# A three-layer graph network on one core: node update and second convolution taken in finished 512-node source chunks inside the edge loop

## The chip, the cores and the metric

One NeuronCore of one Trainium2 chip runs the whole program. The metric is the device time of one execution in microseconds; the runs shown are three, and one further execution was profiled.

## What is computed

3125 nodes of 128 features, 100000 edges sorted by destination, 64 features an edge. Four graph layers follow one another, each with a residual and a LayerNorm. The change concerns the two in the middle.

```python
# layer 1: message network over the edges, then node update
m_input = concat([x[src], x[dst], edge_attr])
h = relu(m_input @ W1 + b1)
messages = relu(h @ W2 + b2)
agg = segment_sum(messages, dst)
x = layernorm(x + layer_norm(x + relu(agg @ Wn + bn), gamma, beta))
# layer 2: convolution with self loops, norm = dinv[row] * dinv[col]
agg = segment_sum(norm * x[row], col)          # edges and one loop per node
x = layernorm(x + layer_norm(agg @ W.T + b, gamma, beta))
# layer 3: h = (1 + eps) * x + segment_sum(x[src], dst); h @ W.T + b; batch norm; relu; residual; layernorm
```

Layers 0, 2 and 3 sum over neighbours by a matrix `adj` of edge counts (25 source tiles of 128 nodes by 3200 destinations, bf16), which the kernel builds first. fp32 rows are split into three bf16 parts (high, middle, low) for these sums.

## The kernel before

The program runs in phases; `phase_end` makes all five engines meet. Every engine has its own instruction stream, written out by hand with semaphores between them.

**Phase 6, the edge loop** (layer 1). 196 blocks of 512 edges, four a loop iteration (`SLOTS`), on every engine a loop over iterations 1 to 47 with a peeled start and end. For each block GpSimd issues four gathers of 128 rows of x @ W1a (`gather`, L602 to L609); before them it waits for the block's index copy (VectorE, `gather_index`, L1446) and for the block four before to be through TensorE's transposes. TensorE's `step` (L865) does, for block b: `hidden_t(b+1)` (L834 transposes the gathered rows, L838 adds the edge part), `inputs_t(b+2)` (L825, transposes the edge features that SP loaded), `sum_nodes(b-1)` (L855), `messages(b)` (L845), `window(b-1)` (L863). ScalarE (`step`, L1124) does `hidden_relu(b+1)` (L1113), `inputs_out(b+2)` (L1108), `take_sums(b-1)` (L1122), `message_relu(b)` (L1117). VectorE (`step`, L1488) does `add_window(b-2)` (L1485: a window of 24 nodes is added into `agg_all`), `gather_index(b+3)`, `block_start(b+3)` (L1473) and `add_bias(b)` (L1479). At the head of each iteration VectorE and SP load four window bases into registers (`bases`). SP issues, per block, the load of 128 KB of edge features (`features`, L463) and a 12 KB load (L492), each once TensorE has used the buffer two blocks back.

**Phase 7** (node update and layer 2). SP loads bn and all of x1 (L510 to L514). TensorE updates seven chunks of 512 nodes (`update`, L902: agg @ Wn plus the bias by an identity matmul, two passes each), VectorE and ScalarE form the residual, two normalizations and the split (`residual`, `norm_1`, `residual_2`, `norm_2`, `less_hi`, `mid`, `less_mid`, L1550 to L1580 and L1156 to L1180), staggered over the chunks; GpSimd adds beta (L624). TensorE sums into the first three destination chunks as sources come (`begin_gcn`, L916), then runs the other four (`aggregate`, L718: 25 source tiles times three parts, 75 matmuls a chunk), adds the self term by transposes (`own_t`, L730, ScalarE copies it, VectorE adds it, L1607) and multiplies by the weight (`gcn`, L934). VectorE ends with node steps (L1617) and groups of two LayerNorms each (`gcn_norms`, L1622), over eight tiles at a time, then four, four and one. SP loads bias, gamma and beta of this layer when the last split is done (L515 to L518).

**Phase 8** is layer 3, with its self term scaled by 1 + eps on ScalarE.

If the input does not suit the windows, a flag (`general`) sends all engines into a fallback (`scan`). That is not taken with this input.

Of the kernel before, what the change touches and what calls it, by code (L numbers as in the profile page):

```python
# [19 lines left out]
F32 = mybir.dt.float32  # L20
# [6 lines left out]
P = 128  # L27
# [8 lines left out]
J = 4  # L36
# [13 lines left out]
SLOTS = 4  # L50
assert NT * WIN_A <= 512 and GRP % 2 == 0
# [9 lines left out]
def build(nc, t, out, x1_d, xa_d, xb_d, table_d):  # L61
    ctx = ExitStack()
    with ctx:
# [8 lines left out]
        arena = sb("arena", [P, 10112], F32)  # L72
# [24 lines left out]
        off = sb("off", [P, 9], F32)  # L97
# [38 lines left out]
        def edge(a, n):  # L136
# [5 lines left out]
        h_t = [edge(o + 2048 + 512 * u, 512) for u in range(2)]  # L142
        msg = edge(o + 3072, 512)
        assert o + 4096 <= 4800
        ec_t = arena[:, 8000:8512]
        w_e = [arena[:, 9024 + 128 * u:9152 + 128 * u] for u in range(2)]
        oh_e = [arena[:, 9280 + 96 * v:9376 + 96 * v].rearrange("p (j w) -> p j w", j=J)
                for v in range(SLOTS)]
        sums = [arena[0:WIN, 9792 + D * u:9792 + D * (u + 1)] for u in range(2)]
# [74 lines left out]
        sums_out = [sem(f"sums_out{v}") for v in range(SLOTS)]  # L224
        win_ready = [sem(f"win_ready{v}") for v in range(SLOTS)]
# [91 lines left out]
        BEGUN = 3  # L317

# [60 lines left out]
        def _(sp):  # L379
# [107 lines left out]

            def edge_loads(i, v, b, last=False):
# [8 lines left out]
            with sp.Else():  # L497
# [12 lines left out]
            sp.dma_start(bias_b[:, :], bcast(t["L1_gnn_bn"])).then_inc(bn_loaded, 16)  # L510
            for c, (k0, nt) in enumerate(CHUNKS):
                sp.dma_start(x1[c], x1_d[k0 * P:(k0 + nt) * P, :].rearrange("(k p) d -> p k d", p=P)
                             ).then_inc(x1_loaded[c > 0], 16)
            sp.dma_start(w_b[:, :], t["L2_gnn_W"]).then_inc(loads[7], 16)  # L514
# [33 lines left out]
        def _(pool):  # L548
# [71 lines left out]
            pool.wait_ge(update_loaded, 48)  # L620
            for c, (k0, nt) in enumerate(CHUNKS):
                x1_wait(pool, c)
                pool.wait_ge(lin_used, 2 * NC + c + 1)
                pool.tensor_tensor(x1[c], x1[c], over(beta_b, nt), ALU.add).then_inc(xb_ready, 1)  # L624
            with pool.If_ne(flag, 0):
                scan(pool, X2, scan_tile)
# [1080 lines left out]
```

## Time and profile before

| what | us |
|---|---|
| runs, median of 3 (lowest, highest) | 1943.5 (1942.7, 1945.01) |
| the profiled execution, its own time | 1940.99 |
| its span, first to last instruction | 1939.0 |
| edge loop, GpSimd's first to last gather | 610.3 to 1592.4 |
| phase 7, first DMA issue to that of phase 8 | 1604.98 to 1782.16 |
| mean granted TensorE clock | 0.967 of full |

Times in the rows are microseconds from the span's start unless marked ns. PE is TensorE's matmul side, PEld its weight loads, DVE VectorE, ACT ScalarE, POOL GpSimd, SP SyncE (SPq its queue); L12 is line 12 of the kernel. An fp32 matmul shows as two passes. What stands in brackets behind a row is how long the engine had been idle and what released it; "issue" is time in which it waited for nothing that the profile shows. Ends of matmuls are modelled.

### The profile page before, as it was taken

The numbers are of one execution on the slowest core, as the hardware profiler recorded it, in microseconds if no ns is written. First come the engines' busy times: TensorE is split into PE (matmuls) and PEld (weight loads), VectorE is DVE, ScalarE is ACT, GpSimd is POOL, SyncE is SP. The second block draws the span as 40 slices with busy tenths as digits, with TensorE's granted clock in tenths as the row PEclk, the third lists the DMA queues.
The fourth block names the chain that finished last, engine by engine and source line by source line (L and its number), as shares of the span: only waits on it lengthen the run. The fifth ranks groups of instructions, "written<-read, shape, count | busy, mean of one in ns | idle before, by whom it ended". The sixth has DMA issues, their size and how long they took to land.

```text
span 1939.0 us, 35472 instructions
## 1 busy us (share of the span) xinstructions
PE 1594.3 (82%) x10363; PEld 1041.1 (54%) x10364; DVE 731.2 (38%) x2702; ACT 692.8 (36%) x1413; POOL 767.6 (40%) x805
## 2 busy tenths in 40 slices
PE   2777777998996888888888888888888884994995
PEld 1444445544555666666666666666666663442444
DVE  7998893112233222222222222222222225365004
ACT  4666663002002443444444444444444445301001
POOL 3000000000003777777777777777777761000000
PEclk9999997999997999999999999999999996997998
DMA  1000000001005333333333333333333321000001
GB/s 54 0 0 0 0 0 3 1 1 38 0 1 141 88 80 82 81 81 81 82 81 80 82 82 80 81 81 81 82 81 82 80 67 38 5 1 2 1 0 34
DMA packets 158346, 93.71 MB, mean 48 GB/s; under 512 B 120529, under 2 KB 143824, under 8 KB 158296
## 3 DMA queue, kind: packets, MB, share of 16 engines
q0 software_dynamic: 25088, 51.43, 10.2%
q1 hardware_dynamic: 133208, 41.60, 8.8%
q8 instruction: 34, 0.56, 0.1%
q14 instruction: 16, 0.13, 0.0%
HBM read 86.44 MB, written 6.52 MB: 48 GB/s over the span
## 4 chain that ended last, share of the span: by engine, by line
POOL 26%; PE 18%; issue 17%; DMA 3%; DVE 3%; ACT 1%; SPq 1%; POOLq 0%; DVEq 0%; ACTq 0%
POOL arena L607 26%; PE ps L726 8%; PE ps L929 3%; DMA arena<-x_w1a,idx 2%; PE ps L845 1%; PE ps L855 1%; PE ps L838 1%; PE ps L834 1%; DVE arena L1335 1%; PE ps L825 1%; DMA x_w1b<-arena 0%; DVE stats L1325 0%; PE ps L863 0%; PE ps L939 0%; PE ps L960 0%
## 5 line engine op out<-in xcount | busy, mean ns | idle before, releaser
L607 POOL DMA_INDIRECT arena<-x_w1a,idx x784 | 740.6, 945 | 832.2 <-issue 824.2
L726 PE MATMUL ps<-adj,arena 128*128 (+2 forms) x1875 | 367.7, 358 | 14.6 <-DVE arena L1300 7.9
L726 PEld LDWEIGHTS ps<-adj,arena 128*128 128x128 bf16 x1875 | 172.1, 99 | 203.2 <-issue 26.0
L1473 DVE TENSOR_TENSOR arena<-win_i,drel 128x96 f32<-128x96 f32 x196 | 50.7, 259 | 554.7 <-PE ps L855 551.3
L1117 ACT ACTIVATE arena<-arena 128x512 f32<-128x512 f32 x196 | 123.6, 631 | 302.6 <-DVE arena L1479 302.6
L834 PE MATMUL ps<-ident_f,arena 128*128 128x128 f32 x784 | 126.7, 284 | 126.1 <-DMA arena<-x_w1a,idx 126.1
L845 PE MATMUL ps<-w_c,arena 128*128 128x128 f32 x1568 | 226.9, 288 | 0.0
L660 PE MATMUL ps<-arena 128*128 128x300 bf16 x784 | 164.8, 296 | 63.1 <-DVE arena L1287 63.1
L1113 ACT ACTIVATE arena<-ps,cols 128x512 f32<-128x512 f32 x196 | 134.8, 688 | 218.2 <-PE ps L838 218.2
L845 PEld LDWEIGHTS ps<-w_c,arena 128*128 128x128 f32 x1568 | 189.7, 191 | 40.1 <-issue 40.1
L855 PE MATMUL ps<-arena 128*24 128x128 f32 x1568 | 206.6, 275 | 2.2 <-ACT arena L1117 2.2
L838 PE MATMUL ps<-arena 88*128 88x512 f32 x392 | 201.8, 596 | 0.0
L1006 ACT ACTIVATE adj<-ps 128x300 f32 x392 | 166.7, 449 | 97.4 <-PE ps L665 91.5
L1287 DVE TENSOR_SCALAR arena<-arena 128x300 bf16<-128x300 int16 x784 | 179.6, 292 | 0.0
L1479 DVE TENSOR_TENSOR arena<-ps,bias_b 128x512 f32<-128x512 f32 x196 | 135.5, 691 | 110.5 <-PE ps L845 110.5
L855 PEld LDWEIGHTS ps<-arena 128*24 128x24 f32 x1568 | 145.5, 102 | 46.2 <-issue 36.7
L834 PEld LDWEIGHTS ps<-ident_f,arena 128*128 128x128 f32 x784 | 83.1, 141 | 144.4 <-issue 82.0
L825 PEld LDWEIGHTS ps<-ident_f,arena 128*88 128x88 f32 x784 | 91.2, 122 | 113.1 <-issue 113.1
L665 PE MATMUL ps<-adj,ident_h 128*128 x392 | 124.6, 318 | 6.7
L660 PEld LDWEIGHTS ps<-arena 128*128 128x128 bf16 x784 | 79.6, 115 | 89.8 <-DVE arena L1287 76.2
L825 PE MATMUL ps<-ident_f,arena 128*88 128x128 f32 x784 | 118.9, 274 | 6.3 <-DVE arena L1473 5.5
L1108 ACT ACTIVATE arena<-ps 88x512 f32<-88x512 f32 x196 | 114.0, 582 | 12.4 <-PE ps L825 8.6
(167 smaller groups left out, 1242.1 us busy)
## 6 DMA issues: line engine op xcount, KB each, us to landing
arena<-in_edge_attr SPq DMA_DIRECT2D x196, 128.0 KB, 2.2
arena<-x_w1a,idx POOLq DMA_INDIRECT x784
arena<-x_w1b SPq DMA_DIRECT2D x196, 12.0 KB
x_spill<-arena SPq DMA_DIRECT2D x1, 1600.0 KB, 7.7
x_w1a<-arena SPq DMA_DIRECT2D x6, 256.0 KB, 2.3
x_w1b<-arena SPq DMA_DIRECT2D x6, 256.0 KB, 2.4
arena<-x_spill SPq DMA_DIRECT2D x6, 256.0 KB, 4.6
out_x<-arena SPq DMA_DIRECT2D x3, 512.0 KB
```

What stands on the lines that cost most here:

```text
L607: pool.indirect_dma_start(out=z_e[v][:, j * D:(j + 1) * D], out_offset=None, in_=xa_d[:, :], in_offset=bass.IndirectOffsetOnAxis(ap=idx[:, ...
L660: last = pe.matmul(ps[:, q, 0:NT * WIN_A], oh_src[v][:, :, j], oh_dst[v][:, j, :], start=(j == 2 * h), stop=False)
L726: last = pe.matmul(ps[:, u, 0:w], parts[q][:, k, :], adj[:, k, bass.ds(c0, w)], start=(k == 0 and q == 0), stop=(k == NT - 1 and q == 2))
L825: last = pe.transpose(ps[0:KE, 0, j * P:(j + 1) * P], ec[v % 2][:, j, :], ident_f[:, :])
L834: pe.matmul(z_t[:, j * P:(j + 1) * P], z_e[v][:, j * P:(j + 1) * P], ident_f[:, :], is_transpose=True, start=(j == 0), stop=False)
L838: pe.matmul(z_t, w_e[v % 2][0:KE, :], ec_t[0:KE, :], start=False, stop=True).then_inc(z_ready[v], 1)
L845: last = pe.matmul(ps[:, 5, j * P:(j + 1) * P], h_t[v % 2][:, j * P:(j + 1) * P], w_c[:, :], start=True, stop=True)
L855: last = pe.matmul(ps[0:WIN, 1, 0:D], oh_e[v][:, j, :], msg[:, j * P:(j + 1) * P], start=(j == 0), stop=(j == J - 1))
L1006: act.activation(adj[:, :, bass.ds(b, WIN_A)], ps[:, q, 0:NT * WIN_A].rearrange("p (k w) -> p k w", w=WIN_A), ACT.Copy).then_inc(adj_writt ...
L1113: act.activation(h_t[v % 2], ps[:, 2 + v % 2, :], ACT.Relu, bias=cols[:, 0:1]).then_inc(h_ready[v], 1)
L1287: last = dve.tensor_scalar(oh_dst[v][:, j, :], iota_c, comb[:, bass.ds(s, 1), j], None, ALU.is_equal)
L1479: dve.tensor_tensor(msg.rearrange("p (j d) -> p j d", d=D), bank(5, J), over(bias_b, J), ALU.add).then_inc(m_sum[v], 1)
```

## The change

- In the loop the iterations are written as: eight plain ones, then five segments of eight (`SEG`; the last has seven), one for each of the first five chunks of 512 nodes, whose destinations no later block touches (`settled`, checked in the preparation by five one-element operations on VectorE that feed the flag). In a segment, iteration r = 0 makes the update of chunk c, iteration r = 1 finishes norms and split, and each of the following ones (r = 2; 29 in all) sums the chunk's four source tiles into one destination chunk u (`partial`: 12 matmuls of 512 columns, in thirds behind the second, third and fourth block). VectorE adds each result to `acc` in SBUF (`take_partial`). Destination chunk 6 (128 columns) is done in the next segment's r = 0.
- The update's x1 chunk comes through one buffer, loaded by SP in iteration r = 1 once VectorE has used the previous one.
- `h_t` and `sums` have one buffer instead of two; ScalarE's step has another order.
- Phase 7 keeps chunks 5 and 6 of the update, one after the other, then sums only those sources (and chunk 4 for destinations 5 and 6) by `gcn_sums`: 15 matmuls a destination, 27 for the last two. VectorE adds `acc` to each (`add_partials`). No self term: `loops` adds the identity to the diagonal blocks of `adj`. The old code stays behind the flag.
- Layer 3's self term is scaled by eps instead of 1 + eps.
- `arena` grows from 10112 to 13248 words a partition; the scratch of the software DMA is set to 4096.

```diff
+EARLY = 5
+SEG = 8
+SEG0 = 9
...
+        def blocks(eng, iteration):
+
+            with eng.Fori(1, SEG0) as i:
+                iteration(i)
+            for c in range(EARLY):
+                i0 = SEG0 + SEG * c
+                iteration(i0, c, 0)
+                iteration(i0 + 1, c, 1)
+                with eng.Fori(i0 + 2, min(i0 + SEG, NB // SLOTS - 1)) as i:
+                    iteration(i, c, 2, i - (i0 + 2))
...
-                with sp.Fori(1, NB // SLOTS - 1) as i:
+                sp.dma_start(w_b[:, :], bcast(t["L1_gnn_bn"])).then_inc(bn_loaded, 16)
+                x1_rows(0)
+
+                def iteration(i, c=None, r=None, u=None):
                     b = bases(sp, base_regs, i)
                     for v in range(SLOTS):
                         edge_loads(i, v, b[v])
+                    if r == 1:
+                        sp.wait_ge(xb_ready, c + 1)
+                        x1_rows(c + 1)
+
+                blocks(sp, iteration)
...
+            def update_tiles(c, some, bank, bias):
+
+                if some[0] == 0:
+                    if c == 0:
+                        pe.wait_ge(update_loaded, 48)
+                        pe.wait_ge(bn_loaded, 16)
+                    if c < EARLY:
+                        b = settled(c)
+                        pe.wait_ge(win_added[b % SLOTS], b // SLOTS + 1)
+                        pe.wait_ge(lin_used, 2 * NC + c)
+                for j in some:
+                    k = CHUNKS[c][0] + j
+                    o = ps[:, bank, j * D:(j + 1) * D]
+                    pe.matmul(o, agg_all[:, k * P:(k + 1) * P], w_a[:, :], start=True, stop=False)
+                    last = pe.matmul(o, ident_f[:, :], bias[:, :], start=False, stop=True)
+                if some[-1] == CHUNKS[c][1] - 1:
+                    last.then_inc(lin_ready, 1)
...
+            def partial(c, u, third):
+
+                w = P if isinstance(u, int) and u == NC - 1 else CH * P
+                if third == 0:
+                    pe.wait_ge(low_ready, 2 * NC + c + 1)
+                    pe.wait_ge(part_added, u + (NC * c + 1))
+                for n in range(4 * third, 4 * third + 4):
+                    j, q = n // 3, n % 3
+                    last = pe.matmul(ps[:, 6, 0:w], up_parts[c][q][:, j, :],
+                                     adj[:, CHUNKS[c][0] + j, bass.ds(u * (CH * P), w)],
+                                     start=(n == 0), stop=(n == 3 * CH - 1))
+                if third == 2:
+                    last.then_inc(part_sum, 1)
...
+                def iteration(i, c=None, r=None, u=None):
+                    for n in range(SLOTS):
+                        step(*at(i, n + 1))
+                        if r == 0 and n < 2:
+                            update_tiles(c, (2 * n, 2 * n + 1), 4, w_b)
+                        if r == 0 and c > 0 and n > 0:
+                            partial(c - 1, NC - 1, n - 1)
+                        if r == 2 and n > 0:
+                            partial(c, u, n - 1)
+
+                blocks(pe, iteration)
...
+                for c, bank in ((NC - 2, 2), (NC - 1, 3)):
+                    update_tiles(c, range(CHUNKS[c][1]), bank, w_b)
+                transposed_weight(loads[7], 16)
+                gcn_sums(0)
+                gcn_sums(1)
+                for u in range(NC):
+                    gcn(2, u, CHUNKS[u][1], sum_t[u % 2])
+                    if u + 2 < NC:
+                        gcn_sums(u + 2)
+                pe.sem_inc(self_ready, NC)
...
-                passed(act, m_ready, i, v, back=2)
-                act.activation(h_t[v % 2], ps[:, 2 + v % 2, :], ACT.Relu, bias=cols[:, 0:1]).then_inc(h_ready[v], 1)
+                passed(act, m_ready, i, v, back=1)
+                act.activation(h_t, ps[:, 2 + v % 2, :], ACT.Relu, bias=cols[:, 0:1]).then_inc(h_ready[v], 1)
...
             def step(i, v, left=2, first=False):
-                if left >= 1:
-                    hidden_relu(*at(i, v + 1))
                 if left >= 2:
                     inputs_out(*at(i, v + 2))
                 if not first:
                     take_sums(*at(i, v - 1))
+                if left >= 1:
+                    hidden_relu(*at(i, v + 1))
                 message_relu(i, v)
...
+            def up_norm_2(c):
+                k0, nt = CHUNKS[c]
+                norm_factors()
+                for j in range(nt):
+                    act.activation(xn[:, k0 + j, :], up_node[c][:, j, :], ACT.Identity,
+                                   scale=rstd[:, CH + j:CH + j + 1], bias=nbias[:, CH + j:CH + j + 1])
+                    last = act.activation(up_node[c][:, j, :], up_node[c][:, j, :], ACT.Identity,
+                                          scale=scaled[:, j:j + 1], bias=scaled[:, CH + j:CH + j + 1])
+                last.then_inc(xs_ready, 1)
+                act.wait_ge(xs_ready, c + 1)
+                if 0 < c < EARLY:
+                    act.wait_ge(part_sum, NC * c)
+                act.activation(up_parts[c][0], up_node[c], ACT.Copy).then_inc(hi_ready, 1)
...
+                def iteration(i, c=None, r=None, u=None):
+                    for n in range(SLOTS):
+                        step(*at(i, n + 1))
+                        if (r, n) == (0, 2):
+                            root(CH)
+                        if (r, n) == (0, 3):
+                            up_norm_1(c)
+                        if (r, n) == (1, 0):
+                            root(CH, CH)
+                        if (r, n) == (1, 1):
+                            up_norm_2(c)
+                        if (r, n) == (1, 2):
+                            up_mid(c)
+
+                blocks(act, iteration)
...
+            def loops(c):
+                for k in range(CHUNKS[c][0], CHUNKS[c][0] + CHUNKS[c][1]):
+                    own.add(dve.tensor_tensor(adj[:, k, k * P:(k + 1) * P], adj[:, k, k * P:(k + 1) * P], ident_h[:, :], ALU.add))
+
+            def up_residual(c, bank):
+                nt = CHUNKS[c][1]
+                dve.wait_ge(x1_loaded[0], 16 * (c + 1))
+                dve.wait_ge(lin_ready, 2 * NC + c + 1)
+                if c > 0:
+                    dve.wait_ge(low_ready, 2 * NC + c)
+                dve.scalar_tensor_tensor(out=up_node[c], in0=bank_of(bank, nt), scalar=0.0, in1=up_x1[c],
+                                         op0=ALU.max, op1=ALU.add).then_inc(lin_used, 1)
+                dve.wait_ge(lin_used, 2 * NC + c + 1)
+                own.add(dve.tensor_tensor(up_x1[c], up_x1[c], over(beta_b, nt), ALU.add))
+                statistics(c, 0, up_node[c])
...
+            def up_residual_2(c):
+                nt = CHUNKS[c][1]
+                dve.wait_ge(normed, c + 1)
+                own.add(dve.tensor_tensor(up_node[c], up_node[c], over(gamma_b, nt), ALU.mult))
+                own.wait()
+                dve.tensor_tensor(up_node[c], up_node[c], up_x1[c], ALU.add).then_inc(xb_ready, 1)
+                dve.wait_ge(xb_ready, c + 1)
+                statistics(c, CH, up_node[c])
...
+            def take_partial(c, u):
+
+                w = P if isinstance(u, int) and u == NC - 1 else CH * P
+                dst = acc[:, bass.ds(u * (CH * P), w)]
+                dve.wait_ge(part_sum, u + (NC * c + 1))
+                if c == 0:
+                    last = dve.tensor_copy(dst, ps[:, 6, 0:w])
+                else:
+                    last = dve.tensor_tensor(dst, dst, ps[:, 6, 0:w], ALU.add)
+                last.then_inc(part_added, 1)
...
+                        if (r, n) == (0, 0):
+                            loops(c)
+                        if (r, n) == (0, 2):
+                            up_residual(c, 4)
+                        if (r, n) == (0, 3):
+                            factors(c, 0)
+                            if c > 0:
+                                take_partial(c - 1, NC - 1)
+                        if (r, n) == (1, 0):
+                            up_residual_2(c)
+                        if (r, n) == (1, 1):
+                            factors(c, CH)
+                        if (r, n) == (1, 2):
+                            up_less_hi(c)
+                        if (r, n) == (1, 3):
+                            up_low(c)
+                        if (r, n) == (2, 3):
+                            take_partial(c, u)
+
+                blocks(dve, iteration)
...
+            with dve.Else():
+                dve.wait_ge(part_added, SUMS_DONE)
+                for c in range(EARLY, NC):
+                    loops(c)
+                    up_residual(c, 2 + c - EARLY)
+                    factors(c, 0)
+                    up_residual_2(c)
+                    factors(c, CH)
+                    up_less_hi(c)
+                    up_low(c)
+                dve.wait_ge(loads[8], 48)
+                gcn_all(add_partials, tail_node, 1)
...
-    nc = _bacc.Bacc("TRN2", target_bir_lowering=False, num_devices=1)
+    nc = _bacc.Bacc("TRN2", target_bir_lowering=False, num_devices=1, dynamic_dma_scratch_size=4096)
```

## Rows read from the trace of the kernel before

**Rows 1.** Busy time by stretch: us, then busy and count of PE, PEld, DVE, ACT, POOL, PE clock.
```profile
640.00:1600.00 960.00, 832.74 (x5376) 605.43 (x5374) 255.89 (x953) 395.87 (x768) 719.42 (x762) 1.00 0.32 80
...
1605.00:1640.00 35.00, 10.86 (x80) 10.67 (x80) 19.40 (x89) 15.75 (x42) 5.07 (x4) 0.65 0.19 52
```

**Rows 2.** Instructions in time order, inside the loop: start, us, engine, line, operation.
```profile
1116.28 0.94 POOL L607 DMA_INDIRECT arena<-x_w1a,idx  x1 [0.30 <-issue]
...
1118.14 0.69 DVE L1479 TENSOR_TENSOR arena<-ps,bias_b 128x512 f32<-128x512 f32 x1 [0.51 <-PE ps L845]
...
1118.84 0.16 DVE L1449 COPY idx<-src_idx 128x4 int32 x1
...
1118.94 0.66 PE L834 MATMUL ps<-ident_f,arena 128*128 128x128 f32 x4 [0.51 <-DMA arena<-x_w1a,idx]
...
1121.81 1.16 PE L845 MATMUL ps<-w_c,arena 128*128 128x128 f32 x8
...
1122.52 0.94 POOL L607 DMA_INDIRECT arena<-x_w1a,idx  x1 [0.30 <-issue]
...
1130.07 0.17 DVE L1449 COPY idx<-src_idx 128x4 int32 x1
...
1132.51 0.94 POOL L607 DMA_INDIRECT arena<-x_w1a,idx  x1 [0.30 <-issue]
```

**Rows 3.** The same view, TensorE in the loop's start-up.
```profile
630.46 0.60 PE L834 MATMUL ps<-ident_f,arena 128*128 128x128 f32 x4
...
634.69 0.66 PE L834 MATMUL ps<-ident_f,arena 128*128 128x128 f32 x4
```

**Rows 4.** The same view, the head of phase 7.
```profile
1604.98 0.36 SPq L510 DMA_DIRECT2D bias_b<-in_L_gnn_bn  x1
1605.38 5.07 SPq L512 DMA_DIRECT2D arena<-x_spill  x7
...
1614.59 0.80 PE L907 MATMUL ps<-w_a,arena 128*128 128x128 f32 x2 [10.02 <-issue]
...
1618.45 0.69 DVE L1556 SCALAR_TENSOR_TENSOR arena<-ps,arena 128x512 f32<-128x512 f32 x1 [13.55 <-PE ps L908]
...
1621.31 1.65 ACT L1159 ACTIVATE arena<-arena,nbias,rstd 128x128 f32<-128x128 f32 x4 [0.45 <-DVE nbias L1541]
```

**Rows 5.** The same view, sums and norms of phase 7.
```profile
1701.27 16.35 PE L726 MATMUL ps<-adj,arena 128*128 128x512 bf16 x75
1701.96 1.65 DVE L1325 BATCH_NORM_STATS2 stats<-arena 128x6 f32<-128x128 f32 x8
...
1715.95 0.69 DVE L1607 TENSOR_TENSOR arena<-ps,arena 128x512 f32<-128x512 f32 x1
...
1718.55 1.13 DVE L1617 SCALAR_TENSOR_TENSOR arena<-ps,dinv,bias_b 128x128 f32<-128x128 f32 x4 [1.91 <-PE ps L939]
...
1759.09 4.35 PE L726 MATMUL ps<-adj,arena 128*128 128x128 bf16 x75
...
1770.03 0.86 DVE L1325 BATCH_NORM_STATS2 stats<-arena 128x6 f32<-128x128 f32 x4
...
1778.22 0.29 DVE L1325 BATCH_NORM_STATS2 stats<-arena 128x6 f32<-128x128 f32 x1
...
1782.16 0.33 SPq L528 DMA_DIRECT2D w_b<-in_L_gnn_W  x1
```

**Rows 6.** The same view, SP's issues across the head of an iteration.
```profile
1005.51 0.32 SPq L492 DMA_DIRECT2D arena<-x_w1b  x1
1007.03 0.38 SPq L463 DMA_DIRECT2D arena<-in_edge_attr  x1
```

**Rows 7.** The page's DMA issues: count, KB each, median us to landing.
```profile
arena<-in_edge_attr SPq DMA_DIRECT2D x196, 128.0 KB, 2.2
...
arena<-x_spill SPq DMA_DIRECT2D x6, 256.0 KB, 4.6
```

**Rows 8.** The same, asked of the stretch from 1600 to 1625 us.
```profile
bias_b<-in_L_gnn_bn SPq DMA_DIRECT2D x1, 64.0 KB, 3.7
```

More of the change, by code:

```diff
@@ L862, in window @@
                 passed(pe, win_added, i, v, back=1)
-                pe.matmul(ps[:, 7, 0:WIN], sums[v % 2], ident_f[0:WIN, 0:WIN], start=True, stop=True).then_inc(win_ready[v], 1)
+                pe.matmul(ps[:, 7, 0:WIN], sums, ident_f[0:WIN, 0:WIN], start=True, stop=True).then_inc(win_ready[v], 1)
             def step(i, v, first=False, left=2):
@@ L1270, in _ @@
             own.add(dve.tensor_reduce(off[0:1, 8:9], falls, mybir.AxisListType.X, ALU.max))
+            for c in range(EARLY):
+                b = settled(c) + 1
+                own.add(dve.tensor_scalar(off[0:1, 9 + c:10 + c], base_row[0:1, b:b + 1], -1.0, float(CH * P * (c + 1)),
+                                          ALU.mult, ALU.add))
             dve.memset(words(0, 3), 0)
@@ L1550, in residual @@
+            phase_end(dve, 6)
+            early = (own.n, roots[0])
+            own.n, roots[0] = before
             def residual(c):
@@ L1595, in scaled_rows @@
                 last.then_inc(gx_ready, 1)
-            with dve.If_ne(flag, 0):
-                scan(dve, X2, scan_tile, before=scaled_rows, after=sums_out(X2))
             def add_self(call, c, read, n_read):
@@ new lines, in _ @@
+            with dve.If_ne(flag, 0):
+                for n in range(NC + 3):
+                    for stage, c in ((residual, n), (residual_2, n - 1), (factors, n), (less_hi, n - 2),
+                                     (factors, n - 1), (less_mid, n - 3)):
+                        if c not in range(NC):
+                            continue
+                        if stage is factors:
+                            factors(c, 0 if c == n else CH)
+                        else:
+                            stage(c)
+                scan(dve, X2, scan_tile, before=scaled_rows, after=sums_out(X2))
+                dve.wait_ge(loads[8], 48)
+                gcn_all(lambda c: add_self(2, c, lin_ready, 3 * NC), node, 0)
+                dve.sem_inc(v_own, NT)
+                own.n += NT
@@ new lines, in _ @@
+            after = (own.n, roots[0])
+            own.n, roots[0] = early
+            with dve.Else():
+                dve.wait_ge(part_added, SUMS_DONE)
+                for c in range(EARLY, NC):
+                    loops(c)
[5 more added lines that the diff above has]
+                    up_low(c)
+                dve.wait_ge(loads[8], 48)
+                gcn_all(add_partials, tail_node, 1)
```

327 lines of the change are left out of this document (194 added, 133 removed).

## The prediction

> **What bounds the kernel now.** I read the busy time by stretch first. From 640 to 1600 us the edge loop runs, TensorE's granted clock is 1.00 (its 2.4 GHz level), and no engine is full: TensorE is busy for 833 of 960 us, GpSimd for 719 [rows 1]. The time-ordered view says who sets the pace. GpSimd issues a gather every 1.25 us (0.94 busy, 0.30 of issue), four to a block, so a block takes 5.0 us whatever the others do. TensorE has been idle for 0.51 us when a block's transposes start, released by the gathered rows, 2.66 us after the block's last gather began [rows 2]. Where rows lay ready and nothing held TensorE, in the start-up, two blocks' transposes are 4.23 us apart [rows 3]. So TensorE has 5.0 - 4.23 = 0.77 us free per block, 3.1 per iteration of four. That is the room into which the change moves work.
>
> How late may TensorE run before GpSimd notices? The gather of block b+3 waits for an index copy that VectorE makes right behind the bias addition of block b-1 (1118.14 + 0.69, copy at 1118.84). Counting copies and gathers in order, a copy ended at 1119.00 for the gather of 1122.52, 3.5 us of room; for the first block of an iteration, where VectorE first loads four registers, it ended at 1130.24 for 1132.51, 2.3 us of room [rows 2]. Only delays beyond 3.5 or 2.3 us lengthen the loop, but those do for good, as GpSimd never idles.
>
> The stage behind the loop runs from 1604.98 to 1782.16, 177.2 us [rows 4, 5]. All of it is chain: update, norms and split, then 25 source tiles for seven destinations, 75 matmuls of 512 columns in 16.35 us each (0.218 a matmul), and the two-LayerNorm groups on VectorE [rows 5].
>
> **The change, part by part.**
>
> *Preparation.* Five one-element operations stand in VectorE's chain ahead of its memsets, about 0.1 us each by the 0.16 of an index copy [rows 2]: +0.4 (0 to 0.8).
>
> *TensorE in the loop.* Three kinds of iteration. In the 29 "rest" iterations a partial sum adds 12 matmuls of 512 columns: 12 x 0.218 = 2.6 against 3.1 free. The iteration needs 4 x 4.23 + 2.6 = 19.5 of 20.0. Fits, barely. In the five first iterations the update adds 16 passes, and (from the second on) the 128-column partial 12 x 0.058 = 0.7 [rows 5]. The update's passes are of the shape of the message matmuls, eight in 1.16 us [rows 2], so 2.3; 3.0 fits into 3.1. The second iteration adds nothing.
>
> *VectorE in the loop.* A rest iteration takes its partial sum behind the fourth block's bias addition: it waits for TensorE's last third (0.3 for the window transpose's two passes, 0.87 for four matmuls, counted from the end of the messages; the bias addition covers 0.7 of it) and adds 0.69. So the next index copy is about 1.3 us later, and this is the one with 2.3 us of room: hidden, 1.0 left. The residual (0.69, 0.69 and statistics of 1.4, within the 2.17 that lie between the residual's end and the first normalization behind the loop [rows 4]) falls on copies with 3.5 of room. Hidden, with 0.1 to 0.7 left. The self loops and factors (under 1 us each) are hidden too.
>
> *SyncE in the loop is where I expect a stall.* At the end of each second iteration SP waits until VectorE has formed x1 plus beta in the residual (`xb_ready`), then issues a 256 KB load, and only then goes on to the next iteration's four registers and its `features`. Unmoved, that load of edge features is out some 8 us before it is needed. Now: with m the end of the messages of block (i,1), VectorE raises `xb_ready` at m + 2.3 (bias 0.69, two additions of 0.7), the x1 issue takes 0.72 (5.07 for seven [rows 4]), registers and the step to the next issue 1.2 (1005.51 + 0.32 to 1007.03 [rows 6]), so `features` starts at m + 4.2 and lands 2.2 later, or up to 4.6 later [rows 7] if it queues behind x1: m + 6.4 to 8.8. TensorE wants it for the transposes of its next step at m + 2.2. Stall 4.2 to 6.6; I take 4.8, near the lower end as only one 256 KB load is ahead of it, where the 4.6 was with seven. Queued behind TensorE are that step's sums and messages; behind those VectorE's bias addition and the index copy.
>
> *ScalarE in the loop.* One step later it runs eight normalizations (four take 1.65 [rows 4], so 3.3) and a conversion (0.7, as any pass of 512 columns) ahead of `inputs_out` and `take_sums`. The relu of block b ends at its m + 1.5, the factors are there by 1.6, the norms are done at 5.6, `take_sums` (behind 0.7 of `inputs_out`) at 6.6. TensorE, back to back, wants it at 4.2 for `window`: 2.4 more.
>
> *What arrives at GpSimd.* Lag: 4.8, less 0.77, plus 2.4, less 0.77 = 5.7 at the iteration's last step; `up_low` adds 0.7 on VectorE; room 2.3. GpSimd slips by 5.7 + 0.7 - 2.3 = 4.1 us. The rest iterations then ask for less than that lag and add nothing. Five segments: **+20 us** (17 with a stall of 4.2, 30 with 6.6; 0 if only ScalarE's stall were there, as 2.4 - 0.77 + 0.7 stays under 2.3 or little above).
>
> *The stage behind the loop.* Written from its start T. TensorE's first update now waits for nothing new. Before, it started 9.6 us after the bias load's issue [rows 4]. 3.7 of them are the load [rows 8]; 5.9 are idle time that no wait explains, with the bulk load of x1 running. The last is bounded by 0 and 5.9 here; I take 2.5, since that bulk is gone. The Trainium skill (Runtime: NRT & Kernel Launch, Instruction fetch mechanics) says that prefetch is sequential and that a taken branch out of the window waits for a fetch; every engine now jumps over the fallback code here, which would make the upper bound the likelier. The jump is in both kernels for TensorE, so the trace neither confirms nor excludes it.
>
> Then chunk 5, serially: update 3.9 (first pass at 1614.59 to the residual's start at 1618.45 [rows 4]; TensorE has idled, and the mean granted clock of those 35 us is 0.65 [rows 1]); residual to first normalization 0.69 + 0.73 + 2.17; normalization 1.65; gamma and beta 1.5; statistics 2.2 + 0.3; second normalization 3.3; four conversions and subtractions 2.8: 15.3. Chunk 6, one tile, behind it: the same steps at about half their length, 7.4 (an estimate, as fixed parts dominate). L = T + 2.5 + 3.9 + 22.7 = T + 29.1.
> SP issues bias, gamma, beta of the last norm only after that; three issues at 0.4 and a landing of 2.7: VectorE starts adding at L + 4.0. TensorE's sums (15 matmuls, 3.3 us a chunk) are ahead of it for chunks 0 and 1. Chunk 0's weight product follows its add (4.8 to 5.9), then chunk 2's sums (to 9.2), then chunk 1's product (10.3) and node step (1.13 [rows 5]): L + 11.5. Then VectorE alone: eight-tile norms 13.95 (1701.96 to 1715.95) twice, two adds and two node steps 3.8, and 3.4 where one add is of one tile, four-tile norms 8.2 twice (1770.03 to 1778.22), the last tile 0.4 + 3.9 [rows 5]. Sum 11.5 + 13.95 + 3.8 + 13.95 + 3.4 + 8.2 + 0.4 + 8.2 + 3.9 = 67.3. 29.1 + 67.3, and 2 for TensorE's slower level in the first sums: 98 (94 to 105). Saved: 177.2 - 98 = **79 us**. TensorE's 40 us of aggregation before the first norms, which were the bound of this stage, stop mattering; late next is VectorE.
>
> *Third layer.* The diagonal makes the scale eps instead of 1 + eps. Same instructions: 0.
>
> **Sum** against the profiled execution of 1940.99 (span 1939.0): + 0.4 + 20 - 79 = 1882.4. The median of the runs is 2.5 above that execution: **1885**.
>
> **The rivals.**
> *A. The loop hides everything.* For it: by TensorE's sums every iteration fits, and the SP stall rests on an order of instructions, not on a row. Against: the wait does stand ahead of `features`. 1943.5 + 0.4 - 79 = 1865.
> *B. TensorE becomes the loop's bound.* The rest iterations leave 0.5 us. If each of six changes between edge work and sums costs 0.2 more (four passes take 0.66 and eight 1.16 [rows 2], so 0.125 a pass and 0.16 to fill), they need 20.7: 29 x 0.7 = 20 on top, 1905. Seen by a mean step over 5.0 in rest iterations. Against: the back-to-back step of 4.23 already holds five changes between unlike matmuls.
> *C. Slower: the gathers wait for descriptor space.* The scratch of the software DMA falls to 4096, from a default left unsaid. If GpSimd must wait for room, it is on the pace-setter: 784 gathers. It decides from 59/784 = 0.075 us a gather; should each wait until its predecessor has landed (2.66 instead of 1.25 [rows 2]), +1.4 x 784 = 1100, so 2980. Against: at most three gathers are in flight at a time. The Trainium skill (DMA: Bandwidth & Descriptors, SWDGE vs HWDGE vs iDMA) has GpSimd append descriptors to rings that live in an SBUF carve-out, so a smaller one can bind; no row shows where.
> *D.* That the change does not do what it says would be the fallback, if a chunk's nodes were not settled in time. Blocks hold about 16 nodes, and the check asks for 512 by block 35: 48 nodes to spare. Excluded.
>
> **How the numbers follow.** Forecast 0.55 (its own range 1872 to 1902: loop 17 to 30, stage 94 to 105), A 0.20, B 0.20, C 0.04, no change 0.01. The range takes A at its lowest stage, 1861, and B with a stage of 103, 1910; outside lie C and the tail of B. A measurement of this kernel tells 0.2% (3.9 us) from nothing. Faster 0.95, same 0.01, slower 0.04.
>
> **What would show it.** GpSimd's gathers stay at 1.25 us, with gaps of 3 to 5 us once per segment, about 160 us apart, five in all (no gaps: A; gaps in every iteration: B; longer spacing everywhere: C). Just ahead of each, a TensorE wait of 4 to 6 us for the edge features at the transposes of L825's counterpart, and one of 2 for ScalarE's sums at `window`. The stage behind the loop: about 98 us, its first norm group some 43 us in, VectorE busy from there on. Wrong I would be if that stage took over 110, or if GpSimd's idle time came from somewhere other than the index copy.

## The result, and the profile after

The changed kernel takes 1896.4 us (1896.3 to 1899.6, 4 runs), the kernel before on the same chip 1943.1: ratio 0.9763, 95% interval 0.9746 to 0.978. Predicted were 1885, range 1861 to 1910. The direction and the range held; 58 us of gain were forecast, 47 came.

First the stage behind the loop. From the timeline of the changed kernel, SyncE, VectorE and TensorE behind the loop (start, duration, then idle time before it and its releaser):

```profile
1636.18 0.34 SPq L534 DMA_DIRECT2D arena<-x_spill  x1
...
1664.37 0.29 DVE L1720 TENSOR_TENSOR arena<-arena 128x128 bf16<-128x128 f32 x1 [0.38 <-ACT arena L1269]
1669.31 1.29 DVE L1848 TENSOR_TENSOR arena<-ps,arena 128x512 f32<-128x512 f32 x2 [4.65 <-DMA beta_b<-in_L_gnn_beta]
...
1676.61 1.64 DVE L1496 BATCH_NORM_STATS2 stats<-arena 128x6 f32<-128x128 f32 x8
...
1735.40 0.33 SPq L590 DMA_DIRECT2D w_b<-in_L_gnn_W  x1
1740.17 0.45 PE L1014 MATMUL ps<-ident_f,w_b 128*128 128x128 f32 x1 [24.62 <-DMA cols<-in_L_gnn_gin_eps]
```

The stage runs from 1636.18 to 1735.40: 99.2 us, where it was 177.2 [rows 4, 5] and 98 was forecast. The last low part ends 28.5 us in (forecast 29.1), VectorE adds 4.65 later (4.0), the first norm group starts 40.4 in (29.1 + 11.5 = 40.6). From there to the end it takes 58.8, where the terms give 55.8 and the forecast held 2 more for TensorE's slower level.

So the shortfall is in the loop. Its waits on TensorE, 600 to 1630 us (us in all, times, longest), and the changed kernel's busy time by stretch (the first of them the whole loop; last columns: TensorE's granted clock, share of the DMA engines, GB/s):

```profile
PE ps L896 <- DMA arena<-x_w1a,idx: 42.7, 66, 1.8
PE ps L887 <- DMA arena<-in_edge_attr: 11.4, 6, 2.7
...
PE ps L925 <- ACT arena L1229: 4.4, 3, 1.5
```

```profile
611.00:1623.00 1012.00, 945.60 (x5935) 671.02 (x5934) 325.46 (x1168) 447.70 (x858) 743.00 (x784) 0.97 0.31 82
...
830.00:837.00 7.00, 5.04 (x34) 3.60 (x33) 3.72 (x10) 5.14 (x12) 5.05 (x5) 1.00 0.17 46
837.00:845.00 8.00, 6.49 (x26) 3.80 (x26) 1.82 (x12) 1.16 (x3) 5.87 (x8) 0.57 0.54 136
845.00:855.00 10.00, 8.47 (x57) 6.17 (x56) 3.89 (x15) 8.10 (x18) 6.26 (x7) 1.00 0.23 61
```

From the first gather to the last the kernel before needs 981.2 us, the changed one 1011.6: +30.4, where +20 was forecast. Setting the start of every gather against the same gather before gives where GpSimd slips (iterations counted by its gathers): 1.6 us once, in the second iteration of the loop; 1.0 to 1.2 in each segment's second iteration (5.3 in all); 2.5 to 5.0 in its third (18.2); 5.3 spread over the rest iterations. The first segment shows how the slips of a second and a third iteration come about. VectorE and GpSimd, then SyncE, then TensorE, and the next late gather:

```profile
826.70 0.68 DVE L1698 SCALAR_TENSOR_TENSOR arena<-ps,arena 128x512 f32<-128x512 f32 x1
...
829.28 0.16 DVE L1622 COPY idx<-src_idx 128x4 int32<-128x4 int32 x1
830.73 0.94 POOL L669 DMA_INDIRECT arena<-x_w1a,idx  x1 [1.45 <-issue]
...
827.99 0.32 SPq L541 DMA_DIRECT2D arena<-x_w1b  x1
837.01 0.38 SPq L534 DMA_DIRECT2D arena<-x_spill  x1
838.39 0.38 SPq L507 DMA_DIRECT2D arena<-in_edge_attr  x1
...
834.85 0.40 PE L925 MATMUL ps<-ident_f,arena 24*128 24x24 f32 x2
837.02 0.85 PE L896 MATMUL ps<-ident_f,arena 128*128 128x128 f32 x4 [1.77 <-DMA arena<-x_w1a,idx]
837.66 1.92 PE L900 MATMUL ps<-arena 88*128 88x512 f32 x2
841.07 1.08 PE L887 MATMUL ps<-ident_f,arena 128*88 128x128 f32 x4 [1.49 <-DMA arena<-in_edge_attr]
842.08 1.90 PE L917 MATMUL ps<-arena 128*24 128x128 f32 x8
...
847.46 0.94 POOL L669 DMA_INDIRECT arena<-x_w1a,idx  x1 [1.65 <-DVE idx L1622]
```

The residual (826.70) holds up the index copy to 829.28, and the gather at 830.73 is 1.15 us late. Those late rows let TensorE, which had caught up, stand idle for 1.77 us. SyncE has issued nothing since 827.99: it waits for VectorE's sum, and the edge features go out at 838.39, for transposes that start at 841.07. That sum does not depend on the late rows, and TensorE, free from 835.25, could have started the features' transposes 1.36 us later by its usual step: the features hold it up by 4.5 us, and the idle 1.77 lies inside that. In all five segments it is 4.4 to 4.6.

In between the granted clock is down, 0.57 of full speed from 837 to 845, most of it at the 1.2 GHz level: the product at L900 takes 1.92 us (before and after it 1.02), the sums at L917 1.90 (1.05). The whole loop has five such stretches, one a segment (837 to 844, 1004 to 1015, 1168 to 1175, 1335 to 1343, 1499 to 1514), and a sixth at 640; the kernel before has none behind 632. The features are equally late in the five segments, but GpSimd slips by 2.6, 4.7, 2.5, 3.5 and 5.0 us in their third iterations, most where the clock stayed down longest (10 and 14 us, in the second and the fifth).

From a copy's end to the gather that it releases, time passes as well. So it was in the kernel before:

```profile
631.27 0.16 DVE L1449 COPY idx<-src_idx 128x4 int32<-128x4 int32 x1
632.24 0.94 POOL L607 DMA_INDIRECT arena<-x_w1a,idx  x1 [2.15 <-DVE idx L1449]
```

That is 0.81 us, and of the 31 gathers of the changed kernel that follow an idle time of over 0.45 us, 21 start 0.80 or 0.81 behind the copy's end and the other ten, each for the last block of an iteration (830.73 above), 1.28 or 1.29.

### The profile page after: what moved, and what is told of

Same layout as the page of the kernel before. It is cut to its first block, busy times and chain, and to the rows that moved or that the text cites. A ratio compares the mean times of both kernels' runs of the same rounds, so it can differ in the third digit from the quotient of the medians.

```text
span 1894.7 us, 35263 instructions
## 1 busy us (share of the span) xinstructions
PE 1607.5 (85%) x10288; PEld 1047.9 (55%) x10289; DVE 761.5 (40%) x2772; ACT 704.0 (37%) x1406; POOL 762.5 (40%) x798
## 4 chain that ended last, share of the span: by engine, by line
PE 25%; POOL 17%; issue 13%; DVE 6%; DMA 5%; ACT 2%; SPq 1%; DVEq 0%; POOLq 0%; ACTq 0%
POOL arena L669 17%; PE ps L788 6%; PE ps L907 4%; PE ps L917 4%; PE ps L900 3%; DMA arena<-x_w1a,idx 3%; PE ps L887 2%; PE ps L896 2%; PE ps L925 1%; DVE arena L1506 1%; PE ps L966 1%; DMA arena<-in_edge_attr 1%; DVE stats L1496 1%; DMA x_w1b<-arena 1%; DVE arena L1516 0%
## 5 line engine op out<-in xcount | busy, mean ns | idle before, releaser
L788 PE MATMUL ps<-adj,arena 128*128 (+2 forms) x1575 | 315.6, 362 | 14.8 <-DVE arena L1471 8.1
L788 PEld LDWEIGHTS ps<-adj,arena 128*128 128x128 bf16 x1575 | 146.1, 99 | 178.8 <-issue 28.1
L907 PE MATMUL ps<-w_c,arena 128*128 128x128 f32 x1568 | 230.8, 291 | 0.0
L917 PE MATMUL ps<-arena 128*24 128x128 f32 x1568 | 211.8, 279 | 2.2 <-ACT arena L1224 2.2
L900 PE MATMUL ps<-arena 88*128 88x512 f32 x392 | 206.3, 608 | 0.0
L917 PEld LDWEIGHTS ps<-arena 128*24 128x24 f32 x1568 | 147.8, 104 | 49.1 <-issue 37.1
L896 PEld LDWEIGHTS ps<-ident_f,arena 128*128 128x128 f32 x784 | 89.9, 143 | 70.2 <-issue 42.0
```

The costliest lines, as they stand in the source:

```text
L788: last = pe.matmul(ps[:, u, 0:w], parts[q][:, k, :], adj[:, k, bass.ds(c0, w)], start=(k == 0 and q == 0), stop=(k == NT - 1 and q == 2))
L896: pe.matmul(z_t[:, j * P:(j + 1) * P], z_e[v][:, j * P:(j + 1) * P], ident_f[:, :], is_transpose=True, start=(j == 0), stop=False)
L900: pe.matmul(z_t, w_e[v % 2][0:KE, :], ec_t[0:KE, :], start=False, stop=True).then_inc(z_ready[v], 1)
L907: last = pe.matmul(ps[:, 5, j * P:(j + 1) * P], h_t[:, j * P:(j + 1) * P], w_c[:, :], start=True, stop=True)
L917: last = pe.matmul(ps[0:WIN, 1, 0:D], oh_e[v][:, j, :], msg[:, j * P:(j + 1) * P], start=(j == 0), stop=(j == J - 1))
```

## The experiments

Theory 1: SyncE's wait ahead of the edge features makes the excess of the loop. Theory 2: the residual's late index copy comes first, and the features wait lies inside what follows (the rows above speak against it: there the wait for late rows lies inside the delay by the features). Theory 3: TensorE's added work. Only `e7` ran on a chip like that of the prediction: the kernel before took 1942 us there, but 2295 to 2317 on the chips of all others (what differs is in the last section). So there only ratios, and waits read in the traces, count; an edit worth under 0.5% doesn't show.

**Late x1 load** (`e1`, and again `e5`, `e8`). SyncE loads a segment's x1 at its head, seven iterations after the sum that it waits for. The load for the first segment stays where it is, ahead of the loop:

```diff
 def iteration(i, c=None, r=None, u=None):      # SyncE
+    if r == 0 and c > 0:
+        sp.wait_ge(xb_ready, c)
+        x1_rows(c)
     ...
-    if r == 1:
-        sp.wait_ge(xb_ready, c + 1)
-        x1_rows(c + 1)
 blocks(sp, iteration)
+sp.wait_ge(xb_ready, EARLY)
+x1_rows(EARLY)
```

> Theory 1 (SyncE's wait): in the changed kernel SyncE waits for the finished node rows before it may issue the next chunk's x1 load, and the edge features queued behind it are late; with the x1 load moved to the head of the next segment nothing is queued behind a wait, TensorE's waits for edge features inside the loop (11.4 us in 6) fall to about 0, its granted clock stays at the upper level, and the loop loses 15 to 20 of its 30 us: 1877 to 1881 us. Theory 2 (VectorE's wait): TensorE is first made idle by a late gather (1.6 to 1.8 us), since the residual on VectorE holds up the copy of the gather's indices, and the features wait only lies inside what follows; then this edit gives under 8 us, 1889 or more. Theory 3 (TensorE's work in the loop is what costs): no change, 1895 to 1898.

> The late x1 load again, since on the chip of the first series the kernel before itself took 2296 us, where transfers and not GpSimd's issues set the loop. On a chip where the kernel before takes 1943: Theory 1 (SyncE's wait): 1877 to 1881 us. Theory 2 (the late gather comes first): 1889 or more. Theory 3 (TensorE's work): 1895 to 1898.

> The late x1 load alone, on a chip where the kernel before takes some 1943 us. Theory 1 (SyncE's wait): the waits for edge features in the loop go and with them most of the loop's excess, 1877 to 1883 us. Theory 2 (the late gather comes first and the features wait lies inside what follows): 1889 or more. Theory 3 (TensorE's work): 1895 to 1898.

**Residual in VectorE's idle time** (`e2`, again `e9`): `up_residual` runs in the same step, but between `gather_index` and `block_start`, where VectorE stands idle for up to 3.6 us.

```diff
 gather_index(*at(i, v + 3))
+if work:                       # up_residual(c, 4) in step (0, 2)
+    work()
 block_start(*at(i, v + 3))
```

> The residual of the node update stands on VectorE between the index copy and the one-hot blocks, in the 3.6 us in which VectorE waits for TensorE anyway, in place of ahead of the next index copy. Theory 1: GpSimd's slip of 1.0 at that place goes, but SyncE's wait and the lower clock stay: 3 to 5 us less, 1891 to 1893. Theory 2: the late gather was the first cause; 12 us less or more, 1884 or below. Theory 3: no change.

> The residual in VectorE's idle time alone. Theory 1: GpSimd's slip of 1.0 at that place goes, SyncE's wait and the lower clock stay: 1891 to 1894 us. Theory 2: 1884 or below. Theory 3: no change.

**Products inside the waits** (`e3`, again `e10`): 4 of TensorE's 128x128 products ahead of `hidden_t` and 10 ahead of `inputs_t` in step (1, 1), into bank 4. For that, TensorE also waits at the head of each segment's second iteration until VectorE's residual has read the bank.

```diff
+spin(fill[0])                  # 4, in step (1, 1) alone
 hidden_t(*at(i, v + 1))
+spin(fill[1])                  # 10
 inputs_t(*at(i, v + 2))
```

> Fourteen extra 128x128 products on TensorE (about 2.1 us at the upper clock), 4 ahead of the gather wait and 10 ahead of the features wait of each segment's second iteration; the waits stay where they are. If the lower clock after the wait is what makes a slip of 2 to 3 us into one of 4 to 6 (five dips of 7 to 14 us with 0.50 to 0.6 granted), the dips go and 5 to 12 us are won: 1884 to 1891. If the wait itself is all of the cost and the lower clock is covered, no change or up to 3 us more: 1896 to 1900.

> Fourteen extra 128x128 products of TensorE inside its two waits in each segment's second iteration. If the lower granted clock behind the wait is what makes the wait dear: 1884 to 1891 us and no stretch at the lower level there. If the wait alone costs: 1896 to 1900, whatever the clock does.

**Both edits** (`e12`, again `e6_both`).

> Both edits, the late x1 load and the residual in VectorE's idle time. Theory 1: 1874 to 1878 (the sum of the two). Theory 2: about what the residual alone gives, within 3 us. If both lie on one chain (either wait alone keeps TensorE idle), the two together give clearly more than the sum of the single gains.

> Late x1 load and residual in VectorE's idle time together, again, for a chip where the kernel before takes some 1943 us and GpSimd's issues set the loop. Theory 1 (SyncE's wait) and theory 2 (the late gather, both waits on one chain) expect 1872 to 1880 us here, with TensorE's granted clock at the upper level throughout the segments; theory 3 (TensorE's work in the loop) expects 1893 or more. Where the kernel before takes some 2296 us again: within 0.3% of the first series' 2284.

Measured, ratio to the kernel before on the same chip with its interval: late x1 0.9913 (0.9884 to 0.9943), 0.9926 (0.9892 to 0.996) and 0.9896 (0.9866 to 0.9926); residual 0.9981 (0.9958 to 1.0003) and 0.9928 (0.9893 to 0.9963); products 0.9982 (0.9961 to 1.0003) and 0.9962 (0.9935 to 0.999); both 0.9939 (0.9912 to 0.9966) and 0.989 (0.9829 to 0.9951). The changed kernel itself was not run there, so no gain over it can be read off; between the edits, the late load is ahead of the residual by 0.7% in the first series and by 0.3% in the last, where the intervals overlap. Both edits together are not ahead of the late load alone there. The times expected where the kernel before takes 1943 us are neither confirmed nor refuted; the one for the other chips (within 0.3% of 2284) came true with 2288.3, though the kernel before took 2317 in that series. What the traces do settle is which edit takes away which wait. TensorE's waits for edge features from 700 us on, with the residual moved (second time), and with the products (second time):

```profile
PE ps L887 <- DMA arena<-in_edge_attr: 28.1, 5, 7.9
```

```profile
PE ps L887 <- DMA arena<-in_edge_attr: 8.5, 4, 2.8
```

Five waits, one a segment, stay when the residual is moved (23.8 us in five the first time). With the late x1 load there is none from 700 us on in any of its five traces, with or without the residual's edit. That much is shown: SyncE's order alone makes the features late. With the products inside, less of the wait is left than with the residual moved; whether the clock then stayed up cannot be told on those chips, since TensorE falls idle there in many other places. That question is open.

**Both, and earlier loads behind the loop** (`e7`). On top: the second GCN's bias is loaded right behind the loop, its gamma and beta behind the last sum of the node update, the third layer's weights and columns ahead of the end of the phase.

```diff
 x1_rows(NC - 1)
+sp.dma_start(bias_b[:, :], bcast(t["L2_gnn_b"])).then_inc(loads[8], 16)
 ...
-sp.wait_ge(low_ready, 3 * NC)
+sp.wait_ge(xb_ready, NC)
 ...
+sp.wait_ge(wt_ready, 1)
+sp.dma_start(w_b[:, :], t["L3_gnn_W"]).then_inc(loads[9], 16)
 ...
 phase_end(sp, 7)
-sp.dma_start(w_b[:, :], t["L3_gnn_W"]).then_inc(loads[9], 16)
```

> Late x1 load, residual in VectorE's idle time, and in the stage behind the loop the loads of the second GCN's bias, gamma and beta ahead of the last low part, and those of the third layer ahead of the end of its phase. The loads' part is independent of the loop: VectorE's wait of 4.65 us for beta falls by 3, TensorE's wait for the third layer's loads (4.8 us behind the phase's start) to under 1: 6 to 8 us less behind the loop on any chip, by the trace 99.2 + 159.3 us to 251 or 252. All together, where the kernel before takes 1943: theory 1 or 2, 1865 to 1874; theory 3, 1887 or more. Where it takes some 2300: 6 to 8 us below the two edits alone.

1873.8 us (1872.0 to 1877.2), against 1942.5 for the kernel before: ratio 0.9651 (0.9634 to 0.9668). That is at the upper end of what theories 1 and 2 expected (1865 to 1874) and far from theory 3 (1887 or more). It beats both kernels: 22.6 us below the changed one, which ran on another chip where the kernel before takes 1943.1. Its busy time in the loop and its timeline:

```profile
611.00:1605.00 994.00, 930.22 (x5927) 660.73 (x5926) 328.65 (x1168) 446.44 (x857) 744.48 (x783) 0.99 0.34 83
...
871.12 0.69 DVE L1734 COPY arena<-ps 128x512 f32 x1 [0.75 <-PE ps L972]
873.02 0.18 DVE L1664 TENSOR_TENSOR arena<-ps,arena 128x24 f32 x1 [1.21 <-issue]
873.26 0.17 DVE L1628 COPY idx<-src_idx 128x4 int32 x1
874.24 0.94 POOL L675 DMA_INDIRECT arena<-x_w1a,idx  x1 [1.86 <-DVE idx L1628]
...
1617.91 0.33 SPq L534 DMA_DIRECT2D arena<-x_spill  x1
1647.51 0.69 DVE L1854 TENSOR_TENSOR arena<-ps,arena 128x512 f32<-128x512 f32 x1 [0.98 <-PE ps L1041]
1715.69 0.47 PE L1020 MATMUL ps<-ident_f,w_b 128*128 128x128 f32 x1 [19.88 <-DVEq L285]
```

First gather to last takes 994.4 us: the excess of 30.4 is down to 13.2, with TensorE's work in the loop unchanged in the code (930 us busy against 946, the clock being higher). So theory 3 explains at most 13.2 of the 30.4. The slips of 1.0 to 1.2 are down to 0.1 or 0.2; those of the third iterations fell from 18.2 to 4.6. The clock inside the loop is back at 0.99, with two short falls (850 to 854, 1160 to 1164).

The slip of 1.6 at 640 is gone too, but neither edit touches anything ahead of it: the first x1 load is issued at the same place, and TensorE waits for edge features behind it in both traces. What differs is the clock. First the changed kernel, then this one:

```profile
638.57 0.64 PE L887 MATMUL ps<-ident_f,arena 128*88 128x128 f32 x4 [1.60 <-DMA arena<-in_edge_attr]
639.14 1.77 PE L917 MATMUL ps<-arena 128*24 128x128 f32 x8
640.84 2.05 PE L907 MATMUL ps<-w_c,arena 128*128 128x128 f32 x8
...
637.31 0.64 PE L893 MATMUL ps<-ident_f,arena 128*88 128x128 f32 x4 [1.36 <-DMA arena<-in_edge_attr]
637.88 1.05 PE L923 MATMUL ps<-arena 128*24 128x128 f32 x8
638.86 1.16 PE L913 MATMUL ps<-w_c,arena 128*128 128x128 f32 x8
```

With 1.77 and 2.05 us for sums and messages GpSimd slips by 1.6, with 1.05 and 1.16 by nothing; the waits ahead differ by 0.24 alone. So a fall of the clock can make a slip where a wait of nearly the same length makes none. (One execution of each, on two chips.) How the 13.6 us that the third iterations gave back divide between SyncE's order, the late gather and the clock is not settled. Most of what is left, 7.9 us (5.3 in the changed kernel), sits in the rest iterations, and the rows show how it comes about: VectorE takes the partial sum (871.12) only once TensorE, by then behind, has made it, then loads four registers (1.21 idle), and the index copy for the next iteration's first block is 1.55 us late at GpSimd. Behind the loop, from the x1 issue to the end, 252.6 us stand against 258.5: 5.9 less, where 6 to 8 were expected.

**Two thirds of the partial sums left out** (`e11`, on top of `e7`) and **one edit per segment** (`e12_mix`).

> On top of the kernel with the late x1 load, the residual in VectorE's idle time and the earlier loads behind the loop (1873.8): in the 29 rest iterations TensorE does only the last 4 of the 12 products of each partial sum; VectorE's copy or addition of all 512 columns stays. Left out are two thirds of the second convolution's sums over the first five chunks. If TensorE's work in the rest iterations is hidden in its free 0.77 us a block, as the prediction has it: 1872 to 1875. If it is not hidden (29 times up to 1.7 us left out): 1840 to 1866.

> One edit per segment of the loop, so that one trace shows each beside the same segment of the changed kernel, where GpSimd slips 3.7, 5.5, 3.8, 4.6 and 6.0 us against the kernel before from the second iteration of a segment to its fourth. Segment 0: x1 load late. Segment 1: residual in VectorE's idle time. Segment 2: 14 extra products of TensorE inside its two waits. Segment 3: x1 load late, and in its rest iterations two thirds of each partial sum's products left out. Segment 4: unchanged. Theory 1 (SyncE's wait): slips of about 1.5 in segments 0 and 3, 4.5 in segment 1, 3.8 in segment 2, 6 in segment 4. Theory 2 (the late gather first): 3 or more in segments 0 and 3, under 2 in segment 1. If the lower clock makes the wait dear: under 2.5 in segment 2. If TensorE's work in rest iterations is not hidden: the drift of 1.9 us in segment 3's rest falls below 0.7. In all, where the kernel before takes 1943: 1887 to 1892.

Both ran where the kernel before takes 2295 to 2316. The first gave 0.9804 (0.9773 to 0.9835), the second 0.995 (0.9926 to 0.9974). Slips of 2 to 6 us a segment cannot be read there, because GpSimd is late by as much in most iterations; the features wait of 4.4 us appears in the segment with the residual moved and one of 2.2 with the products, none where the x1 load was late (nor in the last one, left as it was). Whether the 7.9 us of the rest iterations are TensorE's added products or VectorE's place for taking them stays open. In their steady run the products are hidden: from 900 us on, TensorE of the changed kernel takes 5.1 us for each of three steps with a third and 4.2 for the fourth, 19.5 in all, and waits 0.4 to 0.6 for rows once an iteration. In `e7` the slips beyond 1 us (at 874, 1199 and 1362 us) come in the first such iteration of a segment, where TensorE has no such wait and so is behind; in the other two segments it waits 0.46 and 0.54 there, and the slip is 0.2 and 0.5.

## Why the prediction was right, and where it was short

- **The stage behind the loop**: right, 99.2 for 98, and step by step: TensorE's start at +3.2 (I took 2.5 between 0 and 5.9; what the 3.2 are, the trace does not say), L at 28.5 for 29.1, VectorE's add at 4.65 for 4.0.
- **SyncE's stall**: mechanism, place and count right: five stretches, one a segment, released by edge features, gone when the order is changed. The features held TensorE up by 4.4 to 4.6 us (4.8 forecast). The sign was another, though: TensorE's wait for them shows as 1.4 to 2.7, not 4 to 6, since 1.6 to 1.8 of it is first spent waiting for rows. The term of 4.1 us a segment for what reaches GpSimd measured 3.6 on the mean in the third iterations (18.2 over five), with both stalls in it. That closeness is in part luck: ScalarE's stall was taken too large, which raised the sum, while the room was taken too large and the slower products were left out, which lowered it. What I had not: behind the loads of bn and the first x1, ahead of the loop, features come late as well (1.60), and with the clock down behind that wait 1.6 us were lost.
- **ScalarE's stall** of 2.4: TensorE's waits for its sums are 4.4 us in three, the longest 1.5. Smaller and rarer than forecast.
- **The step that failed is "the residual ... hidden, with 0.1 to 0.7 left"** on VectorE. It is not: the copy comes 2.6 us after the residual's start, and GpSimd slips 1.0 to 1.2 in each segment, 5.3 in all. Two things were wrong with the room of 3.5. It was read where TensorE runs at GpSimd's pace; in that iteration TensorE had just done the update's passes, and the bias addition ended 0.9 us later against the gather than there (2.6 of room by the same count). And it was counted from the copy's end to the gather's start, of which 1.29 us pass in any case for this block. That leaves 1.3 for a copy that came 2.5 later.
- **"The rest iterations ... add nothing"**: they added 5.3 us. The margin of 2.3 ahead of an iteration's first copy was counted from a step in which TensorE was on time, and 0.81 of it is the way from copy to gather: 1.5 were left for 1.3 of delay. The sum for TensorE in these iterations (19.5 of 20.0) was right.
- **TensorE's clock** was in no term of the loop. It fell once a segment, and for 7 to 14 us products took nearly twice as long.
- **The third layer at 0**: from 1735.40 to the end 159.3 us pass, where 156.8 did. 1.8 of the 2.5 are in the first sums, which start 7.24 us into the phase for 6.81 before (0.4) and take longer (1.4), with a granted clock of 0.73 where it was 0.80 over the first 25 us. Before and after:

```profile
1788.97 17.92 PE L726 MATMUL ps<-adj,arena 128*128 128x512 bf16 x75 [1.79 <-DVE arena L1300]
...
1742.64 19.30 PE L788 MATMUL ps<-adj,arena 128*128 128x512 bf16 x75 [2.02 <-DVE arena L1471]
```

No run tried what made the clock lower there.

- **The sum**: 0.7 more at the first gather (0.4 forecast; with the same preparation `e7` has 0.4 less, so it is not told from nothing), 30.4 more in the loop (20) and 0.1 behind it, 78.0 less in the stage (79), 2.5 more in the third layer (0): 44.3 less between the spans, and 46.7 between the medians.
- **The rivals**: A is out (the loop hid nothing like everything), B is out as the main cause (13.2 us at most, not 20 on top; rest iterations in steady run take 19.5 of TensorE, as summed, and not 20.7). C is out: gathers stay 1.25 us apart where no copy is late.

C rested on what the Trainium skill (DMA: Bandwidth & Descriptors, SWDGE vs HWDGE vs iDMA) says of GpSimd: that it appends descriptors to rings in a part of SBUF. With a scratch of 4096 the trace shows no gather held up by a lack of room; no run here shows at what size one would be.

## What to carry to other kernels

Work that is moved beside a paced loop has to fit at the latest copy or load of the loop, at the moment when the engine ahead is behind too, not at its usual one. The room ends not where the released instruction starts but earlier, by the time from the releasing event to that start (here 0.81 to 1.29 us). In an in-order queue a wait stands in front of everything after it: issue the load whose data is needed seven iterations later where its wait has long been met, not ahead of loads that are needed at once, and put side work into the place where the engine idles anyway. Loads of the next stage's constants belong behind the last read of their buffers, not behind the end of the stage.

## What the runs showed of the hardware

Waits of TensorE of less than 2 us, behind an iteration at nearly full use, were followed by products at the 1.2 GHz level, but not each time. In the five segments of the changed kernel it waits 1.77, 1.63, 1.80, 1.61 and 1.62 us for rows. Behind the first, third and fifth the clock falls at once. Behind the other two it stays at the 2.4 GHz level until TensorE has also waited 2.67 and 2.62 us for features, as in the second segment:

```profile
1001.63 0.63 PE L896 MATMUL ps<-ident_f,arena 128*128 128x128 f32 x4 [1.63 <-DMA arena<-x_w1a,idx]
1002.10 1.02 PE L900 MATMUL ps<-arena 88*128 88x512 f32 x2
...
1005.79 1.08 PE L887 MATMUL ps<-ident_f,arena 128*88 128x128 f32 x4 [2.67 <-DMA arena<-in_edge_attr]
```

At the start of the loop it fell behind a wait of 1.60 and not, in `e7`, behind one of 1.36, but there it fell later behind waits of 1.40 and 1.98. The idle 0.5 us in each block of the kernel before never did that [rows 2].

And chips differ. On four of the five chips used in the experiments the kernel before takes 2282 to 2330 us, on the fifth 1940 to 1944. The stages ahead of the loop are as long on both (first gather at 609 to 611 us), and GpSimd's gathers stay 1.25 us apart within a block. But in the loop the engines that wait for TensorE's products start late, now and then by up to 10 us, while TensorE has gone on to its next products. (The expectation of the second late x1 run puts that down to transfers; the rows do not show it.) The late x1 load on such a chip (third time), in order of time:

```profile
1017.90 0.60 PE L889 MATMUL ps<-ident_f,arena 128*88 128x128 f32 x4
1018.43 1.05 PE L919 MATMUL ps<-arena 128*24 128x128 f32 x8
1019.42 1.16 PE L909 MATMUL ps<-w_c,arena 128*128 128x128 f32 x8
1023.31 0.32 SPq L541 DMA_DIRECT2D arena<-x_w1b  x1
1027.43 0.59 ACT L1217 ACTIVATE arena<-ps 88x512 f32<-88x512 f32 x1 [10.07 <-remote]
...
1027.68 0.26 DVE L1648 TENSOR_TENSOR arena<-win_i,drel 128x96 f32<-128x96 f32 x1 [10.82 <-remote]
```

ScalarE and VectorE, which wait for the products of 1017.90 and 1018.43, start within 0.3 us of each other, eight to nine us after these products' ends, and the profile names no releaser on this core. As the ends are modelled, the rows do not tell whether the products or the events were late. The cause was not found.
